# MLP of a transformer block: the second chunk's rows too are turned by VectorE and the DRAM scratch, instead of by TensorE

## What is computed

```
h = layernorm(x, g1, be1) * (1 + scale_msa) + shift_msa
x = x + gate_msa * attention(h)
h = layernorm(x, g2, be2) * (1 + scale_mlp) + shift_mlp
h = gelu(h @ W1 + b1) @ W2 + b2          # 512 -> 2048 -> 512
x = x + gate_mlp * h
out = rmsnorm(x, rms_weight) * (1 + scale) + shift
```

## Time and profile before

| | |
|---|---|
| median of 3 runs | 3703.56 us (3703.33 to 3703.93) |
| the profiled execution, own time | 3704.63 us |
| its span, first to last instruction | 3702.8 us |
| busy in the span | PE 3663.4 us (99%), DVE 2426.5 (66%), ACT 1810.2 (49%), POOL 1959.2 (53%) |
| granted TensorE clock, mean | 0.999 |

### The profile page before, as it was taken

The page is one execution under the profiler, slowest core; times in us unless marked ns, Lnnn a source line. Parts: engine busy times, 40 slices in busy tenths (PEclk is TensorE's granted clock), DMA queues, the critical chain, the costliest instruction groups (busy, mean ns, idle before and its releaser), DMA issues.

```text
span 3702.8 us, 49860 instructions
## 1 busy us (share of the span) xinstructions
PE 3663.4 (99%) x18206; PEld 2615.9 (71%) x18206; DVE 2426.5 (66%) x4163; ACT 1810.2 (49%) x3276; POOL 1959.2 (53%) x636
## 2 busy tenths in 40 slices
PE   8999999999999999999999999999999999999998
PEld 6788885555656566665656565888888888888887
DVE  6677768889898988888988983343333333434442
ACT  3222225667676766666666675433333333333333
POOL 1000116999999999999999997322223222222221
PEclk9999999999999999999999999999999999999999
DMA  8787786667776777777677755112222121222120
GB/s 280 249 273 239 241 253 141 148 142 164 170 164 149 164 171 157 156 161 175 153 160 161 175 130 155 53 63 71 65 91 69 60 69 60 73 68 80 60 69 23
DMA packets 256879, 509.75 MB, mean 138 GB/s; under 512 B 24722, under 2 KB 92306, under 8 KB 240386
## 3 DMA queue, kind: packets, MB, share of 16 engines
q1 hardware_dynamic: 238492, 374.44, 35.4%
q0 software_dynamic: 18144, 132.13, 17.3%
HBM read 240.04 MB, written 132.28 MB: 101 GB/s over the span
## 4 chain that ended last, share of the span: by engine, by line
PE 94%; POOL 2%; DVE 1%; issue 1%; ACT 1%; DMA 1%; SPq 0%; POOLq 0%; DVEq 0%; ACTq 0%
PE psum L740 12%; PE psum L1303 12%; PE psum L1317 12%; PE psum L599 11%; PE psum L601 11%; PE psum L600 11%; PE psum L2018 6%; PE psum L2016 6%; PE psum L2014 6%; PE psum L1348 4%; POOL probs_round L1582 2%; PE psum L1331 2%; ACT probs L1449 0%; DVE max_part L1122 0%; PE psum L749 0%
## 5 line engine op out<-in xcount | busy, mean ns | idle before, releaser
L1122 DVE TENSOR_REDUCE max_part<-psum 128x1 f32<-128x512 f32 x2048 | 1270.3, 680 | 68.7 <-PE psum L740 68.3
L1582 POOL TENSOR_TENSOR probs_round<-probs_round,probs_round 128x2048 f32<-128x2048 f32 x189 | 887.2, 4694 | 104.9 <-PE psum L1317 87.2
L1303 PE MATMUL psum<-q_stack,k_stack 128*128 128x512 f32 x2048 | 767.3, 400 | 0.7 <-ACT probs L1449 0.5
L740 PE MATMUL psum<-k_stack,q_stack 128*128 128x512 f32 x2048 | 754.9, 399 | 0.7
L2228 DVE TENSOR_TENSOR g_parts<-g_full,g_parts 128x512 fp32r<-128x512 f32 x256 | 218.3, 853 | 773.2 <-ACT g_parts L2078 769.7
L1449 ACT ACTIVATE probs_round<-psum 128x512 f32<-128x512 f32 x1024 | 539.1, 604 | 329.7 <-PE psum L1303 327.0
L1449 ACT ACTIVATE probs<-psum 128x512 f32<-128x512 f32 x1024 | 543.9, 605 | 219.7 <-PE psum L1303 205.0
L2075 ACT ACTIVATE g_full<-psum,cols 128x512 f32<-128x512 f32 x256 | 176.6, 690 | 850.9 <-PE psum L601 850.6
L1582 POOL TENSOR_TENSOR probs_round<-probs_round,probs 128x2048 f32<-128x2048 f32 x124 | 571.3, 4608 | 9.7
L2328 POOL TENSOR_TENSOR y_out<-y_out,rows 128x512 f32<-128x512 f32 x60 | 77.3, 1288 | 871.7 <-DVE y_out L2263 871.7
L740 PEld LDWEIGHTS psum<-k_stack,q_stack 128*128 128x128 f32 x2048 | 383.5, 188 | 188.1 <-DVE max_part L1122 113.5
(11 more groups left out here) (200 smaller groups left out, 4923.2 us busy)
## 6 DMA issues: line engine op xcount, KB each, us to landing
probs<-probs POOLq DMA_DIRECT2D x126, 1024.0 KB, 7.8
qk_parts<-qk_out SPq DMA_DIRECT2D x128, 512.0 KB, 4.5
k_stack<-qk_parts SPq DMA_DIRECT2D x96, 512.0 KB, 6.9
q_stack<-qk_parts SPq DMA_DIRECT2D x192, 256.0 KB, 5.7
v_rows<-v_out SPq DMA_DIRECT2D x64, 256.0 KB, 4.1
v_group<-v_rows SPq DMA_DIRECT2D x32, 512.0 KB, 10.1
gated_attention<-gated SPq DMA_DIRECT2D x64, 256.0 KB, 4.7
x<-in_x SPq DMA_DIRECT2D x16, 1024.0 KB, 5.6
```

The costliest lines, as they stand in the source:

```text
L740: pe.matmul(psum[:, bank, :], q_stack[u % 3][0:P, h, i * P:(i + 1) * P], k_stack[G % 2][0:P, h, kh * CH:(kh + 1) * CH], start=True, stop=T ...
L1122: dve.reduce_max(max_part[:, n:n + 1], psum[:, TURNS[at.turn][0], :], AX.X).then_inc(dve_smax, 1)
L1303: pe.matmul(psum[:, ST[n % 3], :], k_stack[G % 2][0:P, h, kt * P:(kt + 1) * P], q_stack[u % 3][0:P, h, :], start=True, stop=True).then_inc ...
L1582: pool.tensor_tensor(total[:, :, :], total[:, :, :], probs(u, kt)[:, :, :], ALU.add).then_inc(pool_sum, 1)
```

## The change

One constant. Only chunk 0 now takes the first way; chunk 1 takes the second, as chunks 2 to 15 did.

```
     HB = 2
     NPC = KM // HB
-    TURNED = 2
+    TURNED = 1
```

## The result

The changed kernel takes 3713.38 us (median of ten runs, 3712.02 to 3733.62; one run of the ten, at a mean clock of 0.947, makes the upper end, and the median does not rest on it), the kernel before in the same comparison 3703.48 us. The ratio is 1.003 with a 95% interval of 1.0022 to 1.0038: **9.9 us slower**, inside the range of the prediction and 0.7 us from its value. The profiled execution took 3712.02 us with a span of 3710.2 us, so it is the quickest of the ten.

What follows compares the result with a forecast made beforehand. TensorE, holding 94% of the chain and never idle in the MLP, was taken as the bound. Terms -1.82 + 8.96 + 2.0 = +9.1 us on 3703.56 gave 3712.7 us, with an 8-in-10 range of 3710.4 to 3716.0.

Steps and rivals of the forecast that it cites:

- the lead: Chunk 0 to 1 boundary: moments start 12.04 us ahead of down tile 15's due time, against 23.83 at the next boundary.
- Transposes, -1.82: TensorE between chunks 0 and 1: removing 16 transposes, all on the bound, gains 1.82 us.
- VectorE's part: Chunk 1's moments, rows and block transposes on VectorE, starting at 2369.88: 8.18 us.
- writes: Four writes of chunk 1's blocks to the scratch and SP's wait for them, ahead of the reads: 6.14 us.
- reads to the last scaling: Chunk 1's four reads from the scratch, from issue to the end of the last two scalings: 6.04 us.
- the low part of tile 14: On VectorE behind the block transposes: ends at 2378.96, 0.24 us before TensorE wants it, so costs nothing.
- The wait, 8.96: TensorE at chunk 0's down tile 15: due 2381.92, stalled until its low part ends at 2390.88, 8.96 us.
- The clock, 2.0: TensorE behind the stall: ten matmuls of down tile 15 at the low clock, 2.0 us more.
- The features: Rival at the chunk 0 to 1 boundary: features arrive in time, only the transposes' gain is left, 3701.7 us; chance 0.02.
- The shorter trip: Rival on the scratch round trip: estimated 8.8 us, stall 2.2 us shorter, 3710.5; shortest read gives 3712.0; chance 0.03.
- The held clock: Rival at down tile 15: the stall comes but the clock holds or returns at once, +7.1 us, 3710.7; chance 0.11.
- The longer loss: Rival: slow write, 1.3 us more, or low clock beyond ten matmuls; 3714.0, up to 3718.5 with both; chance 0.08.

Runs made afterwards that it cites:

- late_second: Kernel before (two chunks turned by TensorE), with chunk 2's moments and rows behind tile 13 of chunk 1 instead of tile 11: 3712.63 us, ratio 1.0024.
- pool_late: Changed kernel, with POOL adding the output bias in the first chunk behind the low part of tile 14 instead of right behind the sums: 3710.98 us.
- three_by_pe: Kernel before with TURNED = 3, so chunk 2 too is turned by TensorE: 3706.24 us, ratio 1.0007.
- filled: Changed kernel with 36 extra matmuls, into a bank nothing reads, between down tiles 14 and 15 of chunk 0: 3710.70 us, ratio 1.0018.
- scale_behind: Changed kernel, with chunk 1's features scaled behind the low part of chunk 0's tile 15 instead of ahead of it: 3710.12 us.
- rows_early: Changed kernel, with chunk 1's moments and rows behind up tile 12 of chunk 0 instead of tile 13: 3710.26 us.
- no_write_wait: Changed kernel, with chunk 1's features read from the turned input xT, not waiting for the scratch writes (outputs are other numbers): 3708.11 us.
- both: Changed kernel with the edits of rows_early and scale_behind joined: 3706.16 us.
- both_woven: The version both, with each feature's low part made one feature behind its scaling instead of all behind all scalings: 3703.83 us, ratio 1.0002.
- both_filled: The version both, with nine extra matmuls, into a bank nothing reads, ahead of chunk 1's first up tile: 3705.20 us.
- woven_pool_late: The version both_woven with the POOL edit of pool_late: 3701.80 us against 3703.53 for the kernel before, ratio 0.9997.

## Why the prediction was right

- **What bounds it, and the lead.** Right: one wait on TensorE's path, never caught up, at a boundary whose chain starts 12 us ahead of the tile that needs it. `late_second` moved the short lead to the next boundary and got a like loss there, 7.2 us of wait. What I had not seen is that part of the short lead is a slow instruction: the moments stand behind a low part that POOL held up by 2.2 us, visible in the kernel before as the 2.86 us of the low part at 2367.10. `pool_late` shows 1.9 us of it.
- **Transposes, -1.82.** `three_by_pe` measures 1.82.
- **The chain's terms.** VectorE's part 8.18 us (predicted 8.18); writes 6.14 (6.14); reads to the last scaling 5.54 (6.04, with 5.29 as the shortest); the low part of tile 14 starts 0.22 us behind the transposes and ends at 2377.97, before TensorE wants it at 2378.07. I had put its cost at nothing; down tile 14 behind it takes 2.82 us instead of 2.72, so it may have cost 0.1.
- **The wait, 8.96.** 8.63 in the profile. The read half was 0.50 us shorter, and the sum had left out the 0.15 us between the end of the low part and the matmul.
- **The clock, 2.0.** 1.60 in the profiled execution, and `filled` shows that it is a cost of its own. That the clock would fall in so long a wait was right, but it fell near 2385.9, 4.9 us after the last matmul was over at 2381.05, and not after 3.3. The runs with long waits had 7 matmuls at the low clock (changed kernel), 9 (pool_late), 10 (scale_behind), 12 (late_second: 5.25 - 2.72 = 2.5 us) and 13 (rows_early, the last of them in the next tile). So ten was a fair middle, and the term varies from run to run. That this variation is why the median lies 9.9 us above the kernel before and the quickest run only 8.5 is argued, not shown: only one execution of each kernel has a profile.
- **The sum.** -1.82 + 8.63 + 1.60 = 8.4, and 8.52 in the stretch; the rest is the 0.1 us of down tile 14. The terms as measured thus add up to less than the 9.1 forecast, while the medians differ by 9.9. Between the two profiled executions and their medians lie 2.5 us, of which 1.14 are the earlier start of down tile 13 and the rest stays open: that the forecast lies within 0.7 us of the median is partly luck.
- **The rivals.** The features were not there in time. The shorter trip is refuted by its own durations: from the first write's issue at 2377.09 to the last scaling's start at 2388.22 it took 11.1 us. By the Trainium skill (DMA: Bandwidth & Descriptors, Anatomy of one DMA) this was an estimated 8.8; the section gives its fit for transfers issued by GpSimd, these are issued by SP, and the trace does not agree. The held clock is refuted by the windows. The longer loss did not come in the profiled execution: the writes took 6.14 us and not 7.44, and seven matmuls were slow, not more than ten. A cause in chunk 0 or in the first use of the scratch is refuted by `late_second` beside the kernel before.
- **Nothing else cost anything**: the eight transfers more, the reordered columns of chunk 1 and the extra work of VectorE are hidden: asked for the whole MLP, the view of the first fence names this one wait of TensorE and no other.

## What to carry to other kernels

Ahead of moving a step off the bound engine, write down two times for it: when its consumer on the bound engine is due, and the length of the whole chain of the new way, from the earliest event that may start it. The gain is the work removed (1.8 us here) only where the lead is longer than the chain; where it is shorter, the difference (9 us) is lost, and a low clock comes on top. The constant that chose the way was not the one that chose the lead: changing `TURNED` alone was a loss, while the same change with the rows a tile earlier, the features woven and POOL moved away was not.

## What the runs showed of the hardware that I had not expected

- **A short wait can bring the low clock, and it comes after the work has resumed.** In the kernel before the clock fell 3.3 us after the last matmul was over the earlier trace rows, and I took a shorter wait to be safe. It was not: behind a wait of 3.0 us (no_write_wait) and of 2.3 us (both) TensorE ran at the full clock for 1.0 and 1.5 us, and then for eight matmuls at the low one. The fall came 3.9 and 3.6 us after the last matmul ahead of the wait was over; in the changed kernel 4.9 us. Behind 0.9 us (both_woven) and behind the 1.24 us that the filling of both_filled left, the clock held. What decides it between these, and whether every execution does the same, was not tried.
- **A small VectorE instruction can wait for POOL as long as a large one.** In the version with the rows early, the addition of 1e-5 to 128x4 numbers took 1.68 us beside POOL's addition over 128x2048 and ended at 2368.29, 0.07 us after POOL's; without POOL beside it, it took 0.17 us (woven_pool_late). The four statistics instructions just before it, beside the same POOL instruction, took 2.47 us for four, as they always do.
